# A two-layer FFN and attention kernel: the turn of an FFN tile and the row loads of four tiles put at other places

## What is computed

```python
x = x + 0.5 * ffn(layernorm(x))       # FFN-1
x = x + attn(layernorm(x))            # 8 batches, one head of 128, causal, rotary
x = x + 0.5 * ffn(layernorm(x))       # FFN-2

# ffn: 16 experts of width 64, top 4 of each token, and one shared expert
scores = sigmoid(xt @ gate_w.T); idx = top_k(scores + gate_b, 4)
comb   = 2.5 * scores[idx] / sum(scores[idx])      # 0 elsewhere
y      = sum_e comb[:, e] * (silu(gate_e(xt)) * up_e(xt)) @ w2_e.T
y     += (silu(gate_s(xt)) * up_s(xt)) @ w2_s.T
```

## Time and profile before

| | us |
|---|---|
| median of 3 runs | 830.62 (827.20 to 832.19) |
| the profiled execution | 829.22 |
| its span in the trace | 827.4, granted TensorE clock 0.996 of full speed |
| PE busy in it | 804.4 |
| POOL, DVE, ACT busy | 622.2, 710.8, 597.0 |

### The profile page before, as it was taken

How to read it: one execution, slowest core, us unless ns; L and a number is a source line. 1 busy time by engine, 2 the same in 40 slices (tenths; PEclk the granted TensorE clock), 3 DMA queues, 4 the chain that set the end, 5 groups by cost and what they waited for, 6 DMA issues and landing times. The chain is left out here.

```text
span 827.4 us, 15760 instructions
## 1 busy us (share of the span) xinstructions
PE 804.4 (97%) x4022; PEld 654.0 (79%) x4022; DVE 710.8 (86%) x2027; ACT 597.0 (72%) x1495; POOL 622.2 (75%) x560
## 2 busy tenths in 40 slices
PE   7799999999999999989999999999999999999998
PEld 6577777777777767879999999767777777777777
DVE  6898999998889988768888887789988899999986
ACT  5777778878776677657767676767777777776664
POOL 6777787777777678688888884377777777787674
PEclk9999999999999999999999999999999999999999
DMA  7467788887777644543334550565667767665653
GB/s 226 131 174 207 196 247 243 239 229 233 226 217 205 202 122 120 156 115 102 95 108 128 141 146 22 148 153 172 182 192 198 199 188 196 189 175 171 173 141 100
DMA packets 93480, 140.83 MB, mean 170 GB/s; under 512 B 10352, under 2 KB 39648, under 8 KB 93408
## 3 DMA queue, kind: packets, MB, share of 16 engines
q1 hardware_dynamic: 93408, 140.03, 60.1%
HBM read 112.67 MB, written 18.93 MB: 159 GB/s over the span
## 5 line engine op out<-in xcount | busy, mean ns | idle before, releaser
L632 POOL TENSOR_TENSOR h_l<-probT,h_h 128x512 fp32r<-128x512 f32 x254 | 337.6, 1335 | 150.7 <-ACT h_h L856 149.0
L1795 PE MATMUL bank<-xh,w_h 128*128 128x512 f32 x545 | 217.4, 399 | 6.6 <-DVE prob L1313 5.4
L856 ACT ACTIVATE h_h<-probT 128x512 fp32r<-128x512 f32 (+1 forms) x285 | 179.2, 629 | 51.3 <-DVE probT L1323 28.8
L1795 PE MATMUL bank<-xh,w_l 128*128 128x512 f32 x545 | 214.6, 394 | 0.0
L1795 PE MATMUL bank<-xl,w_h 128*128 128x512 f32 x545 | 214.3, 393 | 0.0
L919 ACT ACTIVATE bank<-bank 128x512 f32<-128x512 f32 x252 | 146.2, 580 | 70.0 <-PE bank L1795 67.9
L1313 DVE TENSOR_TENSOR prob<-bank,qkT 128x512 f32<-128x512 f32 x252 | 171.3, 680 | 15.1 <-ACT bank L919 10.3
L1323 DVE TENSOR_TENSOR probT<-prob,bank 128x512 f32<-128x512 f32 x255 | 171.2, 671 | 9.1 <-POOL h_l L632 1.7
L1795 PEld LDWEIGHTS bank<-xh,w_h 128*128 128x128 f32 x545 | 102.8, 189 | 40.5 <-DVE prob L1313 10.7
L1795 PEld LDWEIGHTS bank<-xh,w_l 128*128 128x128 f32 x545 | 102.6, 188 | 23.1
L1795 PEld LDWEIGHTS bank<-xl,w_h 128*128 128x128 f32 x545 | 102.8, 189 | 22.1
(11 more groups left out here) (143 smaller groups left out, 1325.2 us busy)
## 6 DMA issues: line engine op xcount, KB each, us to landing
qkT<-comb_rows SPq DMA_DIRECT2D x190, 256.0 KB, 5.1
qkT<-comb_rows SPq DMA_DIRECT2D x124, 128.0 KB, 2.9
rows<-comb_rows SPq DMA_DIRECT2D x28, 512.0 KB, 7.2
stage<-stage SPq DMA_DIRECT2D x64, 128.0 KB, 2.5
X<-in_x SPq DMA_DIRECT2D x16, 256.0 KB, 3.2
stage<-in_x_t SPq DMA_DIRECT2D x16, 256.0 KB, 6.7
x_t<-stage SPq DMA_DIRECT2D x16, 256.0 KB, 4.4
X<-x_rows SPq DMA_DIRECT2D x64, 64.0 KB, 5.3
```

What stands on the lines that cost most here:

```text
L632: nc.gpsimd.tensor_tensor(lo, f, hi.bitcast(F32), ALU.subtract).then_inc(done, 1)
L856: return nc.scalar.activation(dst, src, ACT.Copy)
L1795: return nc.tensor.matmul(dst, lhsT, rhs, start=start, stop=stop)
```

## The change

Four places in the order of two engines' lists, DVE's and SP's. No operation is added or removed, except for one semaphore wait.

1. In `ffn_tile`, for every tile that is neither tile 0 of FFN-1 (which keeps its own branches) nor the last of an FFN, `ffn_h(j)` stands ahead of the scale at j = 6 and of the turn at j = 7.
2. At the start, SP loads x of tile 2 ahead of the second of the three early pieces of w13 (256 KB each).
3. At FFN-1's end, DVE takes v's second sum (`("v", 1)`) ahead of the last residual and the first `attn_max`.
4. `load_x1_rows(12)` and `(13)` go from SP's `attn_batch(0)` into `ffn_first`: one behind the rows of tile 11, one behind the write of tile 14. DVE's wait for the rows stands at i = 5 alone, for 12 tiles in batch 0 and for all 16 in the batches behind it.

```diff
--- before.py
+++ after.py
@@ -428,8 +428,8 @@
             load(gb[:], gate_b, gate_loaded)
             load(w13_f[:, early[0], :], w13T[:, early[0], :], w13_loaded[0])
             load(X[:, NB:2 * NB, :], x_v[:, NB:2 * NB, :], x_loaded[1])
+            load(X[:, 2 * NB:3 * NB, :], x_v[:, 2 * NB:3 * NB, :], x_loaded[2])
             load(w13_f[:, early[1], :], w13T[:, early[1], :], w13_loaded[1])
-            load(X[:, 2 * NB:3 * NB, :], x_v[:, 2 * NB:3 * NB, :], x_loaded[2])
             load(w13_f[:, early[2], :], w13T[:, early[2], :], w13_loaded[2])
             load(w2_f, w2T, w2_loaded)
             load(X[:, 3 * NB:4 * NB, :], x_v[:, 3 * NB:4 * NB, :], x_loaded[3])
@@ -530,9 +530,12 @@
                     write_x1_rows(T - 2, turned[T % 2])
                     if T >= NB:
                         load_x1_rows(T - NB)
+                    if T == TILES - 1:
+                        load_x1_rows(TILES - 4)
                 store_x1(TILES - 2, RING - 2)
                 swap_halves(0, 2)
                 write_x1_rows(TILES - 2, a_turned[0])
+                load_x1_rows(TILES - 3)
                 swap_halves(0, 3)
                 store_x1(TILES - 1, RING - 1)
 
@@ -577,8 +580,6 @@
                 swap_halves(b + 1, 1)
                 if isinstance(b, int) and b == 0:
                     write_x1_rows(TILES - 1, a_turned[1])
-                    load_x1_rows(TILES - 4)
-                    load_x1_rows(TILES - 3)
                     for r in range(RING):
                         sp.wait_ge(xT_moved[r], 32 * TURNS)
                 else:
@@ -1490,13 +1491,13 @@
                     elif step == 4:
                         ffn_rsum(N)
                         ffn_comb(N)
+                    ffn_h(T, q, j)
                     if j == NB + 2 and t + 2 < TILES:
                         ffn_scale(T + 2, base)
                     elif j == PAIRS - 1 and base and t + TURN_AHEAD < TILES:
                         turn_x2(t + TURN_AHEAD, turned[q])
                     elif j == PAIRS - 1 and not base and not first:
                         ffn_turn(T - 1, back)
-                    ffn_h(T, q, j)
                     if step == 0:
                         ffn_logits_turn(N, base)
                     elif step == 1:
@@ -1609,10 +1610,10 @@
                     dve.wait_ge(rope_loaded, 16 * len(ROPE_TILES))
                 ffn_tile(base, turn + TURNS - 1, 3, 1 if start else None)
                 if start:
+                    attn_item(("v", 1), 0, 0, True)
                     residual(TILES - 1, RING - 1)
                     dve.wait_ge(scores_ready, 1)
                     attn_max(0, 0)
-                    attn_item(("v", 1), 0, 0, True)
                     attn_item(("qk", 3), 0, 0, True)
                 else:
                     end_residual()
@@ -1765,8 +1766,8 @@
                                 attn_item(item, b + 1, 1 - p)
                     if first and i == 1:
                         ffn_turn(TILES - 1, RING - 1)
-                    if first and i >= QB - 3:
-                        dve.wait_ge(x_done, ROW_DMAS * (TILES if i == QB - 1 else TILES - 4))
+                    if i == QB - 3 and ahead:
+                        dve.wait_ge(x_done, ROW_DMAS * (TILES - 4 if first else TILES))
                     if i >= QB - 3 and ahead:
                         attn_ln(b + 3, i - (QB - 3))
                     if isinstance(b, int) and B - 3 <= b < B - 1 and i in (4, 6):
```

## The result

The kernel after takes 823.74 us (median of 4 runs, 823.50 to 824.23) against 831.31 us before in the same comparison; the ratio is 0.9916, 95% interval 0.9888 to 0.9943. Timed again beside three experiments it took 823.67 us, ratio 0.993 (0.9911 to 0.9949). The forecast was 823.6. Its total was right; its terms were not all, and one had the wrong sign, as the experiments show.

What follows compares the result with a forecast made beforehand. PE, busy 804.4 of 827.4 us, was taken to bound the kernel, so only its idle counts. Terms -5.2 + 0.3 - 0.5 - 1.3 - 0.3 = -7.0 gave 822.2 from 829.22, 823.6 as median; range 819.8 to 828.6.

Steps and rivals of the forecast that it cites:

- the 5.2 us of the sum: End of batch 0: moving the row loads cuts PE's stretch from 9.11 to 3.87 us; lower bound 3.6.
- the two stalls don't add: End of batch 0: POOL's 4.49 us and DVE's 6.09 us waits lie on one path; PE regains only 5.2.
- The swap of halves 3, +0.3: FFN-1's end, SP queue: tile 13's row loads ahead of this swap cost 0.3 us, bounds 0 and 2.1.
- The rival of a whole group late: Swap of halves 3 waits for all four loads, 2.1 us instead of 0.3: 825.4; included in the forecast's 0.62.
- Part 3, -0.5: FFN-1's end: v's sum falls into DVE's idle time, saving 0.5 us, bounds -0.9 and 0.
- Part 1, -1.3: FFN tiles: scale and turn behind h6 and h7 save 1.3 us, all from held tiles; common tiles nothing on balance.
- the turn's own move costs nothing: FFN tiles: moving the turn costs 0, since its reader is SP's write to DRAM, tiles ahead of use.
- What I gave back: Common tile, PE: the first matmul behind a wait takes 0.50 against 0.40, so 0.1 us comes back.
- the gain in the held tiles: Tiles 1, 12, 13, 17, where POOL holds the scale: 1.3 us gained in all, bounds 0 and 1.7.
- scale held in every tile: Rival, 24 common tiles: 0.3 us each, 7.2 in all, 830.8; up to 0.65 each, 839.2; chance 0.14 (826 to 840).
- Part 2, -0.3: Start: x of tile 2 loaded sooner shortens DVE's 1.42 us wait; 0.3 us gained, bounds -1.4 and +1.4.
- The clock, which I left out of the sum: Start: half-speed clock at 18.20 to 21.50 behind PE's idle; 1.65 us more would go if kept up, not counted.

Runs made afterwards that it cites:

- e1_rows: The kernel before with only the row loads of tiles 12 and 13, and DVE's waits for the rows, moved; 822.54 us, ratio 0.9915.
- e5: The kernel after with the scale put back ahead of h6, the turn staying behind h7; 822.20 us, ratio 0.9922.
- e9: The kernel before with the row loads of tiles 12 and 13 moved, DVE's waits for the rows as before; 823.91 us, ratio 0.9936.
- e11: The kernel after with scale and turn back where they were before, all other changes kept; 822.14 us, ratio 0.9905.
- e3: The kernel before with only x of tile 2 loaded sooner at the start; 829.19 us, ratio 1.0000.
- e4: The kernel before with only v's second sum taken first at FFN-1's end; 829.11 us, ratio 0.9998.
- e10: The kernel before with only DVE's waits for the rows moved, the row loads left where they were; 827.27 us, ratio 0.9969.
- a2_after: The kernel after, unchanged, timed again beside three other runs on one chip; 823.67 us, ratio 0.9930.
- e8_both: The kernel after with scale and turn moved in tiles 1, 12, 17, 28 alone, plus extra unused matmuls in PE's idle time near the start; 821.45 us, ratio 0.9903.
- e2: The kernel before with only scale and turn moved behind h6 and h7; 830.07 us, ratio 1.0015.
- e12: The kernel after with scale and turn behind h6 and h7 in tiles 1, 12, 17, 28 alone; 821.37 us, ratio 0.9899.

## Why the prediction was right, and where not

**What bounds the kernel, and part 4: right.** PE's stretch went from 9.11 to 3.87, which is the 5.2 us of the sum to a tenth, clock included; POOL's and DVE's waits went as said, and the statistics' write is issued 5.8 us sooner (336.43 in e1_rows, 342.20 before). That the 9.11 stood near the mean was some luck, since the four kernels with that stall have 8.43 to 9.30. That the two stalls don't add was right too: alone, the waits' half takes 1.3 off the 9.11 and the loads' half 4.7, together more than there was. By the runs part 4 alone is worth 7.0 us (829.13 - 822.54 = 6.6 by the medians), interval 5.6 to 8.4. The traces show 5.3 of it at batch 0. What is left is not located. FFN-2, from its first router to PE's last matmul, takes 313.2 to 313.7 us in the four kernels with part 1's scale as before and the loads moved (e1, e5, e9, e11) and 313.8 to 314.5 in the four with the loads as before (before, e3, e4, e10); but after and a2_after, one and the same program, have 313.15 and 314.34, so this is not shown to be part 4's.

**The swap of halves 3, +0.3: it costs nothing.** The loads of tile 13 were out 1.6 us ahead of it, and POOL had its data in the same time. The rival of a whole group late did not come. The loads of tile 12, costed at nothing, were free as well: the swap of halves 2 is issued at 319.95 in e1_rows and was at 320.03.

**Part 3, -0.5: right at its place,** 0.54 in every trace, as POOL's idle of 0.47 had told; up to 0.3 of it comes back at batch 0's end in some.

**Part 1, -1.3: wrong in sign, +1.5 and +0.9 by two pairs of runs (the second not clear of noise), +1.7 by one pair of traces and +0.7 by the mean of eleven.** Two steps failed. The first is "the turn's own move costs nothing" in the common tile: only the turn's reader was looked at, and not what comes to stand behind w7. The scale ended where the prediction had it. But h7, now directly behind the w7 that it reads, starts 0.17 later than an instruction that doesn't need w7, so `xl` is 0.84 later in the tile and not 0.65 (208.01 - 208.08 against 205.52 - 206.43, each from the last matmul of up). The router's matmul is 0.41 later instead of 0.29, and the next down product 0.25 instead of 0.09. What I gave back is there, 0.12 for a first matmul without a wait (209.22 to 209.44 instead of 207.32 to 207.66), and little more behind it. About 0.1 a tile stays, 2.1 to 2.3 us over 19 tiles. An edit of that size, times the count of tiles, is a term and no rounding. With the turn left where it was the same sum comes out near nothing, as forecast; that is an estimate from these rows, and no run has that order.

The second is the gain in the held tiles, which I put at 1.3. In the pair a2_after and e11_noA it was larger, 2.7, but 2.3 of it came back in the tiles beside them, and some in tile 2, to which I gave nothing: a tile's PE wait that was removed showed up as the next one's. (I also counted four held tiles; the trace of before has six, 28 and 29 too.) The rival "scale held in every tile" is thus what came, at a third of its price (about 0.11 instead of 0.3 a tile).

The Trainium skill ("SBUF — State Buffer", section "SBUF: two separate sides") has the rule by which the scale is held: the shared port pair goes to whichever of the two starts first, for the whole instruction. The traces agree: tile 9 of after, where the scale comes 0.60 us behind `h_l` and ends 0.56 behind its end, and tile 19 of e8_both, where 0.19 us decide.

**Part 2, -0.3: too small for the runs, and right by the traces as far as they go.** DVE's 1.42 us in the earlier trace rows were read as the kernel's, and they come in four of six executions, as 1.10 to 1.80. Where they come PE waits 0.3 to 0.6 longer; on the mean that is the 0.3. That the size came out so well is luck, since it was a guess between -1.4 and +1.4. The clock, which I left out of the sum, went both ways.

**Why the total fits.** The located terms are -5.3 at batch 0, -0.5 for part 3, -0.3 for part 2 and +0.7 to +1.7 for part 1: -4.4 to -5.4. The runs of after say -7.0 by the ratio (-9.3 to -4.7) and, timed again, -5.8 (-7.4 to -4.2). The forecast's -7.0 lies in both, but the 1.3 us that it gave to part 1 were not there, and part 4's runs gave about 2 us more than its term, most of it not located. The total was better than its terms.

## What to carry to other kernels

Find the queue first: here a write of 0.5 us that others waited for stood in one queue behind 5 us of loads that nobody needed yet, and moving those loads was worth more than all reordering of instructions. An exchange inside a steady tile is to be judged by who meets whom there, and by who then stands directly behind the result that it reads: if two engines can't run at once, being second costs in every tile, so multiply the smallest edge by the count before calling it nothing. Before a wait in a trace is given a price, see in how many executions it comes at all.

## What was not expected of the hardware

The same idle of PE, 3.54 to 3.64 us from matmul to matmul near 25 to 30 us, was followed by the lower clock (0.50) in seven executions (after, e1, e2, e4, e9, e11, e12) and by 1.00 in five (before, e3, e10, a2, e5). a2_after, the same program as after, kept 1.00 and is near 38 us 2.8 us ahead of it; 1.2 of this it had already at tile 1's router, since after had lost the clock behind the first idle as well. The Trainium skill ("TensorE: Matmul & The Clock Gate", Part 1: The HAM clock gate) says that the gate's watch is not tied to the start of a kernel, so that the same kernel differs from run to run; the trace agrees as far as these executions go.

Of one 256 KB load at the start, issued at 4.25 us in each of the six kernels that load x as before, DVE could go on at 9.14 or 9.24 us in two executions and at 10.30, 10.55, 10.62 and 11.01 in the four others.

A VectorE operation of 128x512 that reads the result of the one directly ahead of it started 0.77 us behind that one's start, and one that does not need it 0.60 (w7 and the next, in the median of the common tiles of every kernel with and without part 1's turn).
